# Four early up products of the last stage in the routed stage, three of them behind the last down product

## The reference, cut to what matters

```python
def _moe_forward(x, Wr, br, gate_bias, Wup, bup, Wgate, bgate, Wdown, bdown, Wsu, bsu, Wsg, bsg, Wsd, bsd):
    xt = x.reshape(-1, H)                                # 2048 rows, H = 512
    gate = (xt @ Wr + br) / TEMP                         # 7 experts, 2 chosen for each row
    ...
    u = jnp.einsum('nh,ehi->eni', xt, Wup) + bup[:, None, :]
    g = jax.nn.silu(jnp.einsum('eni,eij->enj', u, Wgate) + bgate[:, None, :]) * u
    eo = jnp.einsum('enj,ejh->enh', g, Wdown) + bdown[:, None, :]
    out = jnp.einsum('ne,enh->nh', probs, eo)
    su = (xt @ Wsu + bsu).reshape(N, NS, I)              # the shared expert, for all rows
    sg = jax.nn.silu(su @ Wsg + bsg) * su
    so = (sg @ Wsd + bsd).sum(axis=1)
    return (out + so).reshape(B, S, H)

def reference(x, ctx_1024, ...):                         # x: 4 x 512 x 512
    x = x + _L0_xattn_ref(_layernorm(x), ctx_1024, ...)  # cross attention, 16 heads
    x = x + _L0_ffn_ref(_layernorm(x), ...)              # _moe_forward
    return x
```

## Time and profile before

| | us |
|---|---|
| median of 3 runs | 993.98 |
| lowest, highest | 993.63, 997.36 |
| profiled execution | 995.3 |
| its span, first to last instruction | 993.6 |
| TensorE busy | 909.5 (92%) |
| VectorE, ScalarE, GpSimd busy | 636.0, 459.5, 563.9 |

### The profile page before, as it was taken

How to read it: one execution, slowest core, us unless ns; L and a number is a source line. 1 busy time by engine, 2 the same in 40 slices (tenths; PEclk the granted TensorE clock), 3 DMA queues, 4 the chain that set the end, 5 groups by cost and what they waited for, 6 DMA issues and landing times. The chain is left out here.

```text
span 993.6 us, 16827 instructions
## 1 busy us (share of the span) xinstructions
PE 909.5 (92%) x5047; PEld 406.6 (41%) x5048; DVE 636.0 (64%) x1019; ACT 459.5 (46%) x846; POOL 563.9 (57%) x487
## 2 busy tenths in 40 slices
PE   3889895799999999989999689999999999999898
PEld 1345442122221222246644245555555555555443
DVE  7888777588787988467776144554554444443388
ACT  3375665678877888722353022332233233323540
POOL 5465556367777775543127499989999920000372
PEclk9798998599999999999999799999999999999999
DMA  7234635445454532133425766666566643335676
GB/s 233 77 92 122 179 105 166 139 158 169 167 177 159 177 105 70 53 107 128 153 112 218 289 191 209 217 200 220 201 215 205 201 139 106 121 109 187 232 203 221
DMA packets 106059, 162.26 MB, mean 163 GB/s; under 512 B 12536, under 2 KB 55608, under 8 KB 105616
## 3 DMA queue, kind: packets, MB, share of 16 engines
q1 hardware_dynamic: 92768, 115.86, 35.9%
q0 software_dynamic: 12896, 45.10, 13.6%
q10 hardware_dynamic: 336, 0.57, 0.2%
HBM read 107.88 MB, written 53.48 MB: 162 GB/s over the span
## 5 line engine op out<-in xcount | busy, mean ns | idle before, releaser
L1089 ACT ACTIVATE p_t<-a_psT 128x512 f32<-128x512 f32 x256 | 138.9, 595 | 47.4 <-PE a_psT L1212 46.1
L1136 DVE TENSOR_REDUCE nm<-quad 128x4 bf16<-128x1984 f32 x60 | 133.9, 2231 | 35.7 <-PE quad L1197 35.7
L1905 ACT ACTIVATE e_xT<-quad 128x512 f16<-128x512 f32 x38 | 22.7, 597 | 229.9 <-PE quad L1969 229.9
L1979 PE MATMUL quad<-w_exp,e_xT 128*128 x456 | 107.2, 386 | 4.9 <-DVE e_xT L1933 2.6
L1039 POOL TENSOR_TENSOR p_sum<-p_t,p_t 128x512 f32<-128x512 f32 x64 | 81.1, 1275 | 53.2 <-ACT p_t L1089 53.0
L1979 PE MATMUL quad<-w_exp,e_uT 128*128 x456 | 104.6, 379 | 0.0
L1979 PE MATMUL e_psY<-w_exp,e_gT 128*128 x456 | 104.6, 379 | 0.0
L1212 PE MATMUL a_psT<-q_stk,k_stk 98*128 98x512 f16 x256 | 84.6, 401 | 11.2 <-ACT p_t L1089 9.4
L215 POOL TENSOR_TENSOR w_exp<-e_raw,w_exp 128x1024 f16<-128x1024 f32 x42 | 91.7, 2184 | 3.5
L1936 DVE SCALAR_TENSOR_TENSOR e_g<-quad,bias 128x512 f32<-128x512 f32 x38 | 26.3, 691 | 85.4 <-PE e_psGT L1969 80.5
L1936 DVE SCALAR_TENSOR_TENSOR e_u<-quad,bias 128x512 f32<-128x512 f32 x38 | 26.3, 691 | 73.9 <-PE quad L1979 73.9
(11 more groups left out here) (338 smaller groups left out, 1797.0 us busy)
## 6 DMA issues: line engine op xcount, KB each, us to landing
xs_dram<-zero SPq DMA_DIRECT2D x38, 256.0 KB, 6.9
bias<-in_L_ffn_bup_dram SPq DMA_DIRECT2D x38, 256.0 KB, 3.3
bias<-in_L_ffn_bgate_dram SPq DMA_DIRECT2D x38, 256.0 KB, 3.4
ys_dram<-e_y SPq DMA_DIRECT2D x38, 256.0 KB, 2.0
e_x<-xs_dram SPq DMA_DIRECT2D x36, 256.0 KB, 2.8
q_dram<-q_st SPq DMA_DIRECT2D x24, 256.0 KB, 3.0
k_dram<-k_st SPq DMA_DIRECT2D x24, 256.0 KB, 3.6
q_stk<-q_dram SPq DMA_DIRECT2D x64, 96.0 KB
```

The costliest lines, as they stand in the source:

```text
L1089: act.activation(probs(w, k), psT[:, k % 2], ACT.Exp, scale=SCALE / (QS * QS)).then_inc(s["exp"], 1)
L1136: dve.tensor_reduce(nm[:, i, :, 0:1].rearrange("p h o -> p (h o)"), psS[:, :, 0:NMAIN], AX.X, ALU.max, negate=True)
L1979: ins = pe.matmul(dst[:, :], stationary, moving, start=(k == 0), stop=(k == len(terms) - 1))
```

## The change

`UP_EARLY` goes from 2 to 4: all four up products of group 0 are made in `routed`. The first stays in step N. The second moves from behind the down product of step N+1 to behind that of step N+2, the last one, and the third and fourth, which stood at the start of `late`, are put behind it. They get the banks psU, psUT and psG. Two waits stand ahead of them, for the last low half of u and the last gate product's eviction. Nothing else is changed; the loop at the start of `late` that made chunks `UP_EARLY` to 3 is empty now.

```diff
-UP_EARLY = 2
+UP_EARLY = 4
...
                     pe.wait_ge(late_ld, 32)
                     pe.wait_ge(g_["split_done"], (E + 1) * (2 * NM) + 2 * NM + 1)
                     pe.wait_ge(s["xT_l"], N)
-                if isinstance(n, int) and N <= n < N + UP_EARLY:
-                    late_up(n - N, (psX, psU)[n - N])
+                    late_up(0, psX)
+                if isinstance(n, int) and n == N + 2:
+                    pe.wait_ge(s["uT_l"], N)
+                    pe.wait_ge(s["g_in"], N)
+                    for c in range(1, UP_EARLY):
+                        late_up(c, (psX, psU, psUT, psG)[c])
```

## The result

Over 22 runs each the changed kernel took 998.34 us (median, 995.01 to 1001.2) and the kernel before 995.62 us (992.79 to 998.57). The ratio is 1.0028 with a 95% interval of 1.0017 to 1.0038: **2.8 us slower**, between 1.7 and 3.8. The prediction had said 2.5 us slower than before, and 996.5 us. The runs of either kernel spread over 6 us, and the two profiled executions differ by 2.4 us before they reach the changed place (block 35's down product, in step N, starts at 908.93 before and at 906.53 after). So the spans, 993.6 and 993.3, compare nothing.

What follows compares the result with a forecast made beforehand. Bound by TensorE's matmuls behind the routed blocks' barrier, with VectorE midway. Barrier +3.35 us, less 2.45 of TensorE's room, plus 1.69 of clock gave +2.6; VectorE's +2.5 on 993.98 made 996.5 us, range 994.0 to 998.6.

Steps and rivals of the forecast that it cites:

- The down products: Last down product waits for ScalarE's copy of its bank, idle about 0.9 us, starting 1.56 us earlier, clock untouched.
- The barrier waits for TensorE's matmuls: Behind the routed blocks, TensorE arrives last once its matmuls end; the barrier opens 3.35 us later.
- Rival B: Barrier does not wait for TensorE's array, opens 1.56 us earlier, nothing stalls; 990.8 us, chance 0.06.
- TensorE's lead and the stall: Behind the barrier TensorE goes on 3.52 us earlier, then stalls 4.2 us for ScalarE's pT copy.
- The clock: The new stall at the pT copy lowers TensorE's clock to 0.50 for some 3.4 us, losing 1.69 us.
- The bounds of 0 to 3.4 us: Clock loss behind the pT stall: 0 if the clock is untouched, 3.4 us if low for two stretches.
- rival C: Behind the pT stall the clock stays low for 10 us, not 3.4, giving +5.9: 999.9 us; chance 0.05.
- Gate products and VectorE: In the late stage the gate products start 2.6 us later and VectorE runs 2.5 us later.
- The end: VectorE's +2.5 us reaches the end of the kernel: 996.5 us against the median.
- The forecast case: Stall of about 4.2 us at the pT copy with one clock loss; range 995.8 to 997.5 us, chance 0.62.
- rival A: Stall at the pT copy without clock loss, or shorter; VectorE sets +1.1 to +1.7 us: 995.3 us, chance 0.22.
- everything the early products gave TensorE is gone at the stall: After the wait for the pT copy, group 1's third up product starts 0.90 us later than before.

Runs made afterwards that it cites:

- e6: Changed kernel with ScalarE copying pT before it waits for the down bias rows and copies them; time ratio 1.0047 to the kernel before.
- e10: Changed kernel with VectorE's gather sums of tiles 0 and 1 cut to 8 columns; 86.2 us from block 35's down product to VectorE's last sum, one run.
- e4: Changed kernel with the third and fourth round of the probabilities' transposes moved behind group 1's last up product; time ratio 1.0046 to the kernel before.
- e5: Changed kernel with 12 extra matmuls (group 1's second up product computed twice) ahead of the wait for the pT copy; time ratio 1.0013 to the kernel before.
- e7: Changed kernel with the second early product left between the last two down products, only third and fourth behind the last; time ratio 1.0017 to the kernel before.
- e8: Kernel before plus two products behind the last down product whose results are thrown away; time ratio 1.0021 to the kernel before.
- e9: Kernel before with SyncE's second and third 1 MB loads held until the second tile's gathered rows landed; time ratio 0.9997 to the kernel before.

## Why the prediction was right, by its own steps

- **The down products.** A wait of about 0.9 us behind the eviction: 0.88, the clock untouched by it.
- **The barrier waits for TensorE's matmuls.** TensorE's entry ended last; 3.35 us later was forecast and 3.39 measured (20.07 against 16.68 from the start of the stretch). Rival B is out. In the trace TensorE's sequencer ran ahead and reached the barrier at 922.3, and its entry held it for 4.1 us, to 926.38, where the last matmul ends at 926.31 (918.38 + 7.93).
- **TensorE's lead and the stall.** The first transposes 3.52 us earlier: 3.48. A stall of 4.2 us at the pT copy: 4.08, and e6 shows its cause.
- **The clock.** 1.69 us forecast (7.03 less 5.34 for 24 matmuls, at a granted clock of 0.50), 1.44 measured in this profile (0.84 in the transposes, 0.60 in the products behind): the stretch of low clock was as long as at the old barrier, 3.4 us, but its first part lay in the stall itself. That it was one such stretch and not two was luck: behind one and the same idle time near 435 the profiles have both. The bounds of 0 to 3.4 us were needed: e10 had 3.0. In the step on rival C I had taken the 24 matmuls at 925.64 as a sign that one stretch of 3.4 us is all that dense work allows; e10 shows two at this very stall. It may be why the timed ratio (2.8 us) lies above the profile's 2.1, but both are inside the interval.
- **Gate products and VectorE.** +2.6 and +2.5 were forecast, +2.16 and +2.18 came (the clock again). That both arrive together held to 0.33 us.
- **The end.** +2.5 forecast, +2.1 in the profile, +2.8 timed. The forecast case by itself had the range 995.8 to 997.5, and 998.34 lies above it, by the kernel before being 1.6 us slower in 22 runs than in the 3; it is inside the stated 994.0 to 998.6 by 0.3 us only. The difference was forecast well, and the time by a margin that luck could have taken.

The weak step was rival A, the forecast without the clock loss, in which VectorE alone decides, at +1.35. For VectorE's own work this was right: e4 gives +1.45 for its first total. But e5, the nearest run to A, with a whole clock and gate products at +1.0, has the first total at +1.95 and the end at +1.9, because gathered rows held VectorE by about 0.5 us, which I had priced at 0.35 at most. So losing no clock would have gained less than A says. Where more of the stall is taken away than A had allowed for (e4 and e6), TensorE waits 5.24 and 3.69 us for VectorE's first total and loses clock there, 2.0 and 1.7 us from the first total to the end; the prediction had no such term, and needed none for the change itself. The statement that everything the early products gave TensorE is gone at the stall is borne out by e7 and e8, which end alike.

What stays open: what decides between 3.4 and 6.8 us of low clock, how often the changed kernel has the longer one at its stall, and what share of the 6 us of spread among the runs of one kernel comes from it.

## What to carry to other kernels

Here work put ahead of a barrier was free only as long as another engine arrived there later; from then on it delayed every engine (the barrier came at 15.1 us with one product behind the last down product, at 17.5 with two and at 20.1 with three), and the engine that did it gained nothing where it soon had to meet one of the others (e7 and e8 both end at 83.4). Before work is moved over a barrier, count for each engine how long behind it the first value is needed that another engine makes, and stop at the amount that the present wait covers (here one product of 2.6 us in a wait of 3.2, where three were put). A lead that could not be used came back as an idle time at the next meeting (4.08 us in the changed kernel, 5.24 in e4). Its clock loss was paid in full where TensorE alone counted from there on (1.7 to 2.0 us in e4 and e6, at VectorE's first total), and less at a meeting ahead of another wait, as at the pT copy: 0.2 us of 1.1 in the changed kernel's profile, 2.2 of 3.0 in e10.

## What the runs showed of the hardware

- In the measured stretch TensorE's clock did not fall at idle times of 0.58, 0.88, 1.72 and 2.35 us, and fell at 3.17, 3.69, 3.96, 4.08, 4.49 and 5.24 us. No limit follows from this: near 50 it fell at 2.38 us in the kernel before. Once it had fallen it was low for 3.4 us in most cases and for 6.8 us in two, e10 (4.49 us) and e4 (5.24 us); in several cases a part of this lay in the idle time itself (clock 0.73 in the 5.10 us of waiting shown for e4).
- TensorE's sequencer reached the barrier well ahead of its engine, by 3.4 us before and by 4.1 with the change, and waited there until its last matmul had ended: its entry ended at 922.57 before and at 926.38 with the change, the last matmul at 922.47 and at 926.31. With the change it was 0.2 us from then to ScalarE's first instruction.
- The bias rows, six loads of 2 and 14 KB issued at the same moment as three loads of 1 MB, landed 7.3 to 8.3 us behind the barrier where ScalarE waited for them and all three were issued, and 6.1 us behind it with two of the three big loads held back (ScalarE's wait ended at 928.88 behind a barrier at 922.76 in e9).
